# Attention with routed experts on one core: the values' product in two pieces at odd steps, mask products of 64 columns, one tile fewer per segment

## The reference, cut to what matters

```
Q, K, V = heads(x @ Wq), heads(x @ Wk), heads(x @ Wv)     # 16 heads of 8
scores  = where(key > query, -1e6, Q @ K.T / sqrt(8))      # 512 x 512 per head
x = layernorm(x + softmax(scores) @ V @ Wo + bo)
xn = layernorm(x) * gamma + beta
two best of 8 experts per row, gates from the softmax of xn @ Wg
x = layernorm(x + sum over the two of gate * (gelu(xn @ W1[e] + b1[e]) @ W2[e] + b2[e]))
```

## Time and profile before

| what | value |
|---|---|
| median of 3 runs | 992.43 us (990.83 to 999.39) |
| the profiled execution | 994.34 us, span 992.5 us |
| PE busy | 873.5 us, 88% of the span |
| DVE busy | 740.1 us, 75% |
| ACT busy | 677.9 us, 68% |
| POOL busy | 653.6 us, 66% |
| mask products, line 1154 | 1536 matmuls, 121.0 us |
| values' product, line 1171 | 2048 matmuls, 180.2 us |

### The profile page before, as it was taken

How to read it: one execution, slowest core, us unless ns; L and a number is a source line. 1 busy time by engine, 2 the same in 40 slices (tenths; PEclk the granted TensorE clock), 3 DMA queues, 4 the chain that set the end, 5 groups by cost and what they waited for, 6 DMA issues and landing times.

```text
span 992.5 us, 29037 instructions
## 1 busy us (share of the span) xinstructions
PE 873.5 (88%) x9185; PEld 566.2 (57%) x9185; DVE 740.1 (75%) x2029; ACT 677.9 (68%) x1434; POOL 653.6 (66%) x907
## 2 busy tenths in 40 slices
PE   4689899998999989999999999769999999998960
PEld 2334444444444444544444444359999988998860
DVE  1877779888988888888888888855554555458867
ACT  1277687777787777877777877746666555667763
POOL 6243555778678777777787786667767656556652
PEclk9799999999999999999999999989999999999995
DMA  7614635636446355345354342253233323266644
GB/s 198 194 66 158 176 92 165 175 107 203 123 146 203 100 172 167 103 155 171 99 165 147 101 145 61 79 143 87 79 81 89 86 75 89 74 206 193 209 110 146
DMA packets 169379, 132.50 MB, mean 134 GB/s; under 512 B 52938, under 2 KB 155377, under 8 KB 169104
## 3 DMA queue, kind: packets, MB, share of 16 engines
q1 hardware_dynamic: 156880, 112.48, 38.5%
q0 software_dynamic: 8704, 17.06, 5.1%
q10 hardware_dynamic: 3648, 1.12, 0.5%
HBM read 71.55 MB, written 61.15 MB: 134 GB/s over the span
## 4 chain that ended last, share of the span: by engine, by line
PE 37%; POOL 8%; issue 6%; ACT 5%; DVE 5%; DMA 1%; ACTq 1%; SPq 0%; DVEq 0%; POOLq 0%
PE ring L1235 12%; PE ring L1251 11%; PE ps_v L1171 3%; POOL probs L666 2%; PE ring L1108 2%; DVE negmax L1282 2%; ACT probs L798 2%; PE ring L1139 2%; POOL rs L732 1%; POOL rows_d L708 1%; PE ps_v L1225 1%; ACT probs L937 1%; DVE probs L1624 1%; PE ring L1154 1%; ACT vpad L922 1%
## 5 line engine op out<-in xcount | busy, mean ns | idle before, releaser
L1282 DVE TENSOR_REDUCE negmax<-ring 128x2 f32<-128x1024 f32 (+3 forms) x512 | 409.5, 814 | 70.5 <-PE ring L1154 67.5
L798 ACT ACTIVATE probs<-ring 128x768 f32<-128x768 f32 (+1 forms) x384 | 334.7, 878 | 114.0 <-PE ring L1108 107.9
L666 POOL TENSOR_SCALAR_AFFINE_SELECT probs<-probs 128x512 f32<-128x512 f32 x256 | 162.8, 639 | 159.5 <-ACT probs L798 157.7
L922 ACT ACTIVATE vpad<-ring,b_s 128x128 f32<-128x128 f32 x576 | 164.5, 370 | 113.5 <-PE ring L1235 111.1
L716 POOL DMA_INDIRECT y_d<-vpad,xs x144 | 146.3, 1016 | 99.1 <-DVE vpad L1593 54.9
L1171 PE MATMUL ps_v<-probs,vpad 128*32 128x512 f32 (+3 forms) x2048 | 180.2, 441 | 8.3 <-POOL probs L666 8.3
L1235 PE MATMUL ring<-vpad,w_t 128*128 128x128 f32 x1152 | 156.0, 279 | 8.7 <-ACT vpad L945 5.8
L1251 PE MATMUL ring<-qarea,vpad 128*128 x1152 | 155.0, 278 | 3.3 <-issue 3.0
L1235 PEld LDWEIGHTS ring<-vpad,w_t 128*128 128x128 f32 x1152 | 141.7, 194 | 11.1 <-ACT vpad L945 7.2
L708 POOL DMA_INDIRECT rows_d<-xn,slot x128 | 128.6, 1005 | 28.4 <-issue 25.1
L1251 PEld LDWEIGHTS ring<-qarea,vpad 128*128 128x128 f32 x1152 | 140.0, 192 | 7.8 <-issue 6.5
(11 more groups left out here) (190 smaller groups left out, 1170.0 us busy)
## 6 DMA issues: line engine op xcount, KB each, us to landing
kside<-qk_d SPq DMA_DIRECT2D x32, 512.0 KB, 5.5
qk_d<-qarea SPq DMA_DIRECT2D x32, 384.0 KB, 2.7
xs<-rows_d SPq DMA_DIRECT2D x144, 66.0 KB, 1.9
qk_d<-qarea SPq DMA_DIRECT2D x32, 256.0 KB, 2.4
qarea<-qk_d SPq DMA_DIRECT2D x16, 512.0 KB
qodd<-qk_d SPq DMA_DIRECT2D x16, 512.0 KB
probs<-y_d SPq DMA_DIRECT2D x16, 512.0 KB, 4.5
xin<-L_attn_x SPq DMA_DIRECT2D x16, 256.0 KB, 3.8
```

The lines of the kernel that those rows point to most:

```text
L666: pool.affine_select(out=diag, in_=diag, pattern=[[0, 4], [1, P]], compare_op=ALU.is_ge, fill=0.0, base=0, channel_multiplier=-1).then_inc ...
L798: nc.scalar.activation(of_unit(h // 2, part), ring[:, 2 * part % 3, :, (0, P, P)[part]:S], ACT.Exp, scale=SCALE).then_inc(sem("exp_done"), 1)
L922: ins = nc.scalar.activation(ht[:, n % 4, c, :], ps_a[:, n % 4, c * P:(c + 1) * P], ACT.Gelu_apprx_tanh, bias=b1_s[:, bass.ds(e, 1), c:c + ...
L1282: ins = nc.vector.tensor_reduce(negmax[:, n // 6 % 2, qb, s:s + 2], ring[:, (2 * n + 1) % 3, :, c0:c0 + nk], AX.X, ALU.max, negate=True)
```

## The change

Three things. First, the values' product of a group comes in two pieces, both at odd steps: blocks 0 and 3 (512 and 128 queries) at step 1, blocks 1 and 2 (384 and 256) at step 3; the piece of step 2 is gone. Second, the mask products of the maxima have 64 columns in place of 128 (and 2 x 64 in place of 2 x 128); their number stays. Each masks one 64 x 64 triangle on the diagonal. The corner that they leave out (the first 64 queries of a block against its last 64 keys) is masked by the score product itself: a spare row of the query side is 1 on the first half of a query block, and the same row of the key side is -1e30 on the last half of that key block. These rows are set once, at the start, by a POOL iota, five small DVE operations and the same two DMAs per parity as before. Third, `TILES` is one less per segment, 103 and 39.

```diff
-    TILES = [n * TOPK // P + E for n in SEG]
+    TILES = [n * TOPK // P + E - 1 for n in SEG]
...
-                             fill[:, :] if what else across(fill[:, 1], 2)).then_inc(sem(f"filled{par}"), 16)
+                             fill[what][:, :]).then_inc(sem(f"filled{par}"), 16)
...
-            sp.wait_ge(sem("fill_set"), 2)
+            sp.wait_ge(sem("fill_set"), 4)
...
+            pool.iota(past_i[:, 0], pattern=[[1, 2 * QB]], base=2 * P, channel_multiplier=-2).then_inc(
+                sem("past_rows"), 1)
...
                         to = ring[:, (2 * n + 1) % 3, half, :]
-                        past = pastb[rows, at:at + P]
+                        past = pastb[rows, HALF:P]
                         if n % 3 == 2:
-                            to = to.rearrange("p (a n) -> p a n", n=P)[:, 0:QB:QB - 1, :]
-                            past = past.unsqueeze(1).broadcast_to([HALF, 2, P])
+                            to = to.rearrange("p (a n) -> p a n", n=P)[:, 0:QB:QB - 1, HALF * c:HALF * (c + 1)]
+                            past = past.unsqueeze(1).broadcast_to([HALF, 2, HALF])
                         else:
-                            c1 = (QB - 1 - n % 3) * P
-                            to = to[:, c1:c1 + P]
+                            c1 = (QB - 1 - n % 3) * P + HALF * c
+                            to = to[:, c1:c1 + HALF]
                         ins = pe.matmul(to, diagb[rows, at:at + P], past, start=False, stop=(c == 1))
...
-                    if h % 4:
+                    if h % 2:
                         vb, vg = (i, h // 4 - 1) if h >= 4 else (i.plus(-1), 3)
-                        values(vb, vg, ((0,), (1,), (3, 2))[h % 4 - 1])
+                        values(vb, vg, ((0, 3), (1, 2))[h % 4 // 2])
...
+            dve.wait_ge(sem("past_rows"), 1)
+            nc.vector.tensor_scalar(past_i[:, 1], past_i[:, 0], 2 * HD - 1, None, ALU.bitwise_and).then_inc(
+                sem("past_rows"), 1)
+            dve.wait_ge(sem("past_rows"), 2)
+            for what in range(2):
+                nc.vector.tensor_scalar(past_f[:, what], past_i[:, 1], float(what), NEG if what else 1.0, ALU.is_equal,
+                                        ALU.mult).then_inc(sem("past_rows"), 1)
+            for what in range(2):
+                dve.wait_ge(sem("past_rows"), 3 + what)
+                nc.vector.tensor_copy(fill[what][:, 1].rearrange("p (j n) -> p j n", n=HALF),
+                                      along(past_f[:, what], HALF)).then_inc(sem("fill_set"), 1)
```

More of the change, by code:

```diff
@@ L203, in build_program @@
         flat = probs[:, :, :].rearrange("p r n -> p (r n)")
-        fill = xc[:, :, :].rearrange("p q d -> p (q d)").bitcast(BF16).rearrange("p (r n) -> p r n", r=2)
+        fill = [t[:, :, :].rearrange("p q d -> p (q d)").bitcast(BF16).rearrange("p (r n) -> p r n", r=2)
+                for t in (x2, xc)]
+        past_i = sb("past_i", [P, 2, 2 * QB], I32)
+        past_f = sb("past_f", [P, 2, 2 * QB])
         y_t = flat[:, 0:8 * S].rearrange("p (r n) -> p r n", r=4)
@@ L1271, in _ @@
         def _(dve):
-            nc.vector.memset(fill[:, 0], 1.0).then_inc(sem("fill_set"), 1)
-            nc.vector.memset(fill[:, 1], 0.0).then_inc(sem("fill_set"), 1)
+            nc.vector.memset(fill[1][:, 0], 1.0).then_inc(sem("fill_set"), 1)
+            nc.vector.memset(fill[0][:, 0], 0.0).then_inc(sem("fill_set"), 1)
+            dve.wait_ge(sem("past_rows"), 1)
[9 more added lines that the diff above has]
+                                      along(past_f[:, what], HALF)).then_inc(sem("fill_set"), 1)
             def maximum(b, n, part):
```

## The result

The changed kernel takes **1003.97 us** (median of 8 runs, 999.19 to 1007.41), the kernel before, run beside it, 995.74 (8 runs, 990.83 to 999.40): a ratio of 1.0081, with a 95% interval of 1.0053 to 1.0110. That is inside one per cent, as forecast, and 6 us above the predicted 998, at the upper end of the forecast's own range (988 to 1004). The forecast was reckoned from a median of 992.43 us for the kernel before; against the 995.74 measured beside it the change costs 8.2 us, where the sum had 5.3. The profiled execution has a span of 997.4 us, where before had 992.5; it is the fastest of the eight.

What follows compares the result with a forecast made beforehand. PE, busiest at 88%, was taken to wait for ACT at odd steps and POOL at step 1. +0.68 us per iteration gave +9.5, tiles -4.2, sum +5.3: 998 us predicted, 8-in-10 range 974 to 1009, forecast's own 988 to 1004.

Steps and rivals of the forecast that it cites:

- The prices: A mask pair costs 0.11 us with 256 columns, 0.055 with 128, half that with 64; 128 values' columns cost 0.21.
- steps 2, 3 and 10, 11: M2 stays where ACT sets it and the moved values' work runs behind it: +0.31 and +0.26 us per iteration.
- 4, 5: S1 and M2 come 0.055 us earlier, then 0.11 less for masks and 0.21 more behind M2: +0.05 per iteration.
- 12, 13: Masks gain 0.055 us twice and 0.11, the values' product loses 0.21: 0 per iteration.
- 14 to 1: POOL's chain holds step 1's values' product but for 0.055 us; it then takes 1.21 in place of 1.00: +0.16 per iteration.
- The mechanism: At steps 3 and 11 M2 waits for ACT's exponential of S1; the values' piece before step 3's M2 only filled PE's wait.
- steps 6 to 9: -0.10: PE gains about 0.4 us, but S2 of step 9 waits for DVE; the four steps get about 0.1 shorter per iteration.
- The third rival: DVE stays behind through steps 8 and 9 and S2 is late there: +0.35 us per iteration, 1003 us; chance 0.04.
- The tiles' -4.2: Two fewer of 144 tiles, 2.10 us each, on PE's path in that stage: -4.2 us.
- Three signs named in advance: PE's idle time at step 1 above 0.54 us; new idle before M2 at steps 7 and 15, some 0.4 to 0.9, ACT-ended.
- PE's list paid back: M2 goes as soon as PE reaches it, so PE's shorter list saves time: 950 us, half paid back 971 to 973; chance 0.21.
- Masks that do not get shorter: Weight loads keep the mask products' spacing: 1003 us if M0 and M1 gain nothing, 1011 if M2 neither; chance 0.20.

Runs made afterwards that it cites:

- e1: The kernel before with the 64-column mask products and their spare rows only, values' product and tiles as before: 991.26 us, ratio 0.9960.
- e5: The kernel before with the 384-column piece of the values' product (steps 2, 6, 10, 14) left out altogether: 993.03 us, ratio 0.9972.
- e2: The kernel before with the values' product in two pieces at the odd steps, masks and tiles as before: 1017.42 us, ratio 1.0212.
- e4: The changed kernel with POOL's multiplication by gamma one place later, behind the mask of step 6 in place of step 5: 995.67 us, ratio 0.9995.
- e8: The changed kernel with DVE's small product of the gates half a step earlier in DVE's list, ahead of POOL's multiplication: 998.79 us, ratio 1.0019.
- e3: The changed kernel with the values' product in three pieces as before, so the masks and the tiles alone: 988.35 us, ratio 0.9927.
- e11: The changed kernel with SP's loads of the second half of the next block's sides held back until step 4's maxima are in place: 1003.86 us, ratio 1.0077.
- e10: The kernel before with SP's loads of the second half of the next block's sides held back until step 4's maxima are in place: 989.49 us, ratio 0.9951.

## Why the prediction was right, and where it was wrong

**What held.** The prices: four masks of 64 columns cover 0.22 us, the two-block masks 0.28; steps 2, 3 and 10, 11 lost 0.27 and 0.29 where 0.31 and 0.26 were forecast, 4, 5 lost 0.12 for 0.05 (M2 came 0.09 earlier, but the 0.11 behind it was not gained, as in e1), 12, 13 nothing, 14 to 1 0.12 for 0.16. The mechanism: at steps 3 and 11 M2 stayed with ACT, shown by e5, where PE's work was taken away and M2 did not move, and by e2 (M2 at 2.87 and 3.34 behind S0, with 0.49 and 0.86 us of idle time). PE's busy time fell by 31 us and the attention ended 10.5 later. The start cost nothing to be seen: the first S0 came 3 us earlier in this trace. In the nine traces with the new work at the start it stands between 37.3 and 40.5, in the four without it between 39.2 and 41.2; why is open.

**The step that failed** is the term "steps 6 to 9: -0.10". It measured +0.66, which makes the iteration +1.46 in place of +0.68. The prediction kept DVE "as late as its list makes it" and priced that list at the durations of before. (Its own terms there, 0.1 to 0.15 and 0.11 gained and 0.21 lost, come to between 0 and -0.05, not to -0.10; that is small beside the miss.) It did not ask what POOL does beside DVE: an operation of 0.18 us started 0.12 us ahead of a POOL operation of 1.28, and a shift by 0.4 us of one list against the other put it behind. e4 and e8 show that this is the whole of the miss: with the two taken apart, from either side, steps 6 to 9 come within 0.05 of the forecast's time. The third rival, DVE late through steps 8 and 9, had the right place, for a wrong reason and with 0.04 too small a chance. Its 1003 us matches the time by luck: its +0.35 for one iteration is half of the 0.76 that steps 6 to 9 cost beyond the forecast.

The Trainium skill has the rule, in "SBUF — State Buffer", section "Who interferes with whom": "A DVE instruction with two SBUF inputs contends with a GpSimd instruction that reads SBUF", and the same section calls the shared port pair an exclusive lock, with issue order deciding who blocks. The traces agree: 0.15 us alone, 1.02 behind a multiplication of 1.27, both ending together; while the product with one input in PSUM, at 325.49 in before, takes 0.19 beside the multiplication, and the maximum from PSUM takes 1.23 both beside it (changed kernel, from 325.89 to 326.25) and ahead of it (before, where it ends at 325.15).

**The term that was missing.** The kernel before loses time to the transfer of the maxima, which comes late in some iterations (table of waits, 150 to 578 us, of before and then of after):

```profile
PEld ring L1108 <- DMA qarea<-mt: 3.2, 4, 1.1
...
PEld ring L1108 <- DMA qodd<-mt: 2.4, 3, 1.4
```

```profile
PEld ring L1113 <- DMA qodd<-mt: 1.6, 2, 1.1
...
PEld ring L1113 <- DMA qarea<-mt: 0.4, 1, 0.4
```

A change that makes steps 2 and 3 longer gives the transfer that time; one that makes them shorter, as e1 and e3, meets it more often. That is part of why the masks alone gained 4 us, and by the traces most of why the change cost 8 and not 14. The books close roughly: 14 iterations by 1.46 are 20.4, against 13.6 from the first S0 to the first tile; less the tiles' 6.0 they give 14.4. e11 has 14.4 over e10 by the medians (1003.86 less 989.49), and 16.7 between the two profiled spans (1003.6 less 986.9). Some 6 of the 14.4 were hidden in the measured 8.2 by the waits that went. The tiles' -4.2 was -6.0 by the traces of before and after, -3 by the medians of e1 and e3, no more than their noise.

So the time came out within 6 us of the forecast in part because two misses lie on opposite sides: +0.76 for one iteration from the port, and the transfer's waits; that part is luck.

Three signs named in advance failed too: PE's idle time at step 1 is 0.42 and not more than 0.54, though the product comes as late as forecast; at step 7 there is only 0.1 us before M2 (326.64 to 326.74) and not 0.4 to 0.9; and at step 15 DVE and not ACT holds PE.

**The other rivals.** PE's list paid back: ruled out by e5. Masks that do not get shorter: ruled out by the 0.22 us. The Trainium skill, in "TensorE: Matmul & The Clock Gate", section "LDWEIGHTS (loading the stationary operand)", gives the time of a weight load by the columns of the weights alone. Taken as a bound on the masks, as in the prediction, it does not hold here: the traces have four of them in 0.22 us where four covered 0.27 with the same weights.

## What to carry to other kernels

Before you move a piece of work, look at what the next instruction on its engine waits for: here work in front of such a wait was free up to the wait's end, and behind it cost its full length (0.43 and 0.39 for 0.42 us of work in e2), even on the engine with the highest busy share. A list that shifts by some tenths of a microsecond against another can make a tiny operation many times longer, so check which DVE operations with two inputs in SBUF come near POOL's long ones, and put them apart in the lists. And look for transfers that land just in time: they hide what a slower version costs and eat what a faster one gains; here moving two bulk loads by a few microseconds was worth about as much (5 to 7 us) as the masks with them in the way (4 us).

## What was not expected of the hardware

DVE's product of 4 columns took between 0.15 us (e4, mean of 12) and 1.03 (e8, mean of 12; 0.94 in the changed kernel), by nothing but what POOL ran beside it. A transfer of 16 KB that was issued 3 to 6 us behind four of 512 KB let PE go on only 4.9 us after its issue (e3), and steps 2 and 3 took 6.20 us there in place of 5.09; with two of the four held back by some 6 us, nearly all such waits went.
